# Loading x ahead of adj, first chunk two blocks at a time, and single loads behind each tanh, in a two-layer graph kernel on one core

## The reference

```
filt = tanh(adj * adj) * (adj > 0);  new_adj = the 350 largest of each row
h2   = tanh(x @ W_proj + b_proj);    x1 = layernorm(x + relu(new_adj @ (h2 @ W_gcn) + b_gcn))
node = [(adj > 0) @ x1, (adj < 0) @ x1] @ node_W + node_b * diag(adj)
edge = (adj @ x1) @ edge_W + edge_b * diag(adj)
out  = layernorm(x1 + node + edge)
```

## Time and profile before

| | |
|---|---|
| median of three runs | 616.18 us |
| the profiled execution, its time and its span | 615.21 us, 613.4 us |
| PE busy | 603.1 us, 98% of the span |
| DVE, ACT, POOL busy | 471.4, 418.2, 186.8 us |
| DMA | 130.65 MB, mean 213 GB/s |
| granted TensorE clock | 0.999 of full |

### The profile page before, as it was taken

One profiled execution on the slowest core, in us unless ns is written; L12 is line 12 of the kernel. 1 busy time (PEld: TensorE's weight loads), 2 busy tenths in 40 slices (PEclk: granted clock), 3 DMA queues, 4 the chain that ended last, 5 costly groups with the idle time before them and its releaser, 6 DMA issues.

```text
span 613.4 us, 5755 instructions
## 1 busy us (share of the span) xinstructions
PE 603.1 (98%) x1986; PEld 344.0 (56%) x1986; DVE 471.4 (77%) x681; ACT 418.2 (68%) x299; POOL 186.8 (30%) x80
## 2 busy tenths in 40 slices
PE   7999999999999999999999999999999999999996
PEld 6644444444444444455555655655655656557995
DVE  2677979788887979986787697796796786886743
ACT  2676786868687686648884783883983883875950
POOL 0398697888879797100000000000000000000000
PEclk9999999999999999999999999999999999999999
DMA  8999999999999980047898399388487595784000
GB/s 238 311 348 347 345 322 325 264 324 299 323 271 302 321 205 0 2 137 205 231 247 241 106 253 252 102 244 226 133 238 194 162 249 154 193 248 124 2 18 18
DMA packets 141181, 130.65 MB, mean 213 GB/s; under 512 B 9443, under 2 KB 141158, under 8 KB 141158
## 3 DMA queue, kind: packets, MB, share of 16 engines
q1 hardware_dynamic: 74982, 66.22, 38.8%
q10 hardware_dynamic: 66176, 64.17, 37.5%
HBM read 128.27 MB, written 2.10 MB: 213 GB/s over the span
## 4 chain that ended last, share of the span: by engine, by line
PE 97%; DMA 1%; SPq 0%; ACT 0%; DVE 0%; issue 0%; ACTq 0%; DVEq 0%
PE acc L988 36%; PE acc L1002 34%; PE stage L1011 10%; PE stage L1010 10%; PE stage L1002 2%; PE to_rows L1017 1%; PE to_rows L1016 1%; DMA x_rows<-in_x_dram 1%; PE stage L956 1%; PE to_rows L973 1%; PE stage L962 1%; SPq L378 0%; PE to_rows L948 0%; PE to_cols L962 0%; PE stage L951 0%
## 5 line engine op out<-in xcount | busy, mean ns | idle before, releaser
L630 DVE STREAM_TRANSPOSE a_cols<-a_rows 128x2048 f32<-128x2048 f32 x128 | 294.6, 2306 | 91.9 <-PE stage L1011 53.0
L988 PE MATMUL acc<-a_cols,rhs 128*128 128x512 f32 x512 | 221.4, 592 | 0.8 <-ACT a_cols L559 0.7
L1002 PE MATMUL acc<-a_cols,x_rows 128*128 128x512 f32 (+1 forms) x512 | 216.2, 565 | 0.0
L367 POOL TENSOR_TENSOR a_cols<-a_cols 128x1536 f32<-128x1536 f32 x64 | 175.3, 2748 | 61.5 <-DVE a_cols L630 60.6
L988 PEld LDWEIGHTS acc<-a_cols,rhs 128*128 128x128 f32 x512 | 96.6, 190 | 119.9 <-issue 119.9
L559 ACT ACTIVATE a_cols<-a_cols 128x2048 f32<-128x2048 f32 x64 | 122.3, 1912 | 49.2 <-POOL a_cols L367 48.0
L1002 PEld LDWEIGHTS acc<-a_cols,x_rows 128*128 128x128 f32 x512 | 96.0, 189 | 86.3 <-issue 81.0
L579 ACT ACTIVATE a_rows<-a_rows 128x4096 f32<-128x4096 f32 x32 | 115.9, 3623 | 25.6 <-DVE a_cols L630 12.3
L1010 PE MATMUL stage<-masks,x_hi 128*128 128x512 f32 (+1 forms) x288 | 126.8, 449 | 0.0
L582 ACT ACTIVATE a_rows<-a_rows 128x4096 f32<-128x4096 f32 x32 | 116.0, 3624 | 1.0
L1011 PE MATMUL stage<-masks,x_lo 128*128 128x512 f32 (+1 forms) x288 | 103.1, 367 | 0.0
(11 more groups left out here) (107 smaller groups left out, 235.7 us busy)
## 6 DMA issues: line engine op xcount, KB each, us to landing
a_rows<-in_adj_dram ACTq DMA_DIRECT2D x120, 512.0 KB, 10.1
a_rows<-in_adj_dram SPq DMA_DIRECT2D x120, 512.0 KB, 9.0
out_dram<-n_rows SPq DMA_DIRECT2D x28, 64.0 KB, 8.4
x_rows<-in_x_dram ACTq DMA_DIRECT2D x6, 128.0 KB, 4.5
x_rows<-in_x_dram SPq DMA_DIRECT2D x6, 128.0 KB, 6.2
x_rows<-in_x_dram ACTq DMA_DIRECT2D x4, 64.0 KB, 2.2
x_rows<-in_x_dram SPq DMA_DIRECT2D x4, 64.0 KB, 2.1
diag<-in_adj_dram SPq DMA_DIRECT2D x16, 1.0 KB
```

Of the source, the lines that this page charges most:

```text
L367: nc.gpsimd.tensor_tensor(part, part, part, ALU.mult).then_inc(squared_pool, 1)
L630: nc.vector.transpose(half_out(hs), half_in(s, h % HALVES)).then_inc(turned[layer], 1)
L988: last = nc.tensor.matmul(acc[parity][:], rhs[:, b, :], a_cols[:, h % HSLOTS, k, :], start=(b == 0), stop=(b == BLOCKS - 1))
L1002: last = nc.tensor.matmul(sums, x_rows[:, b, :], rows(a_cols[:, h % HSLOTS, k, :]), start=(b == 0), stop=(b == BLOCKS - 1))
```

## The change

- x is loaded whole ahead of adj, in six parts of 4, 4, 4, 4, 8 and 8 blocks. W_proj goes ahead of part 1 on SP's queue; b_proj has a semaphore of its own; b_gcn moves from ACT's queue to SP's, behind the four pieces of chunk 0.
- The head runs its 8 groups in one regular order; the eight matmuls of ones are gone; DVE makes all copies of turned x, ACT one more copy of `rhs`. Two halves instead of three are turned before the head ends.
- In chunk 0 each half is worked as two pairs of blocks: two transposes, two squares on POOL and on ACT, two tanhs, and PE waits for each pair.
- From chunk 1 on ACT issues one quarter after each tanh, never two.
- At the end the last two tiles have a PSUM bank each; their sums are copied, weighed and taken into the statistics one by one.

Layer 1 up to its last two tiles is as before; apart from the ones no product with data is added or left out, and the bytes loaded are the same.

```diff
-X_PARTS = [4, 4, 8, 8, 8]
-X_FIRST = 4
+X_PARTS = [4, 4, 4, 4, 8, 8]
...
-KEEP_WARM = 8
-EARLY = [("rhs", 4), ("rhs", 5), ("rhs", 7)]
+PAIR = HB // 2
+PAIR_POOL = PAIR * CH * 3 // 4
+EARLY = [("rhs", 5), ("rhs", 6)]
...
-last_rows = [to_rows[:, 0:PARTS[0][1], :],
-             acc_m[1 - LAST[2]][:, 0:PARTS[1][1] * F].rearrange("p (t f) -> p t f", f=F)]
+last_rows = [[to_rows[:, k, :] for k in range(PARTS[0][1])],
+             [acc_m[1 - LAST[2]][:, 0:F], stats_at[:, 0:F]]]
...
 GROUPS = BLOCKS // TILES
-X_LAST = sum(X_PARTS[:X_FIRST]) // TILES
...
 USES = turns[:2]
-for k in range(X_LAST):
-    USES += hids[k:k + 1] + rhss[max(k - 2, 0):max(k - 1, 0)] + turns[:X_LAST][k + 2:k + 3]
-USES += rhss[X_LAST - 2:X_LAST - 1] + turns[X_LAST:X_LAST + 1] + rhss[X_LAST - 1:X_LAST] + turns[X_LAST + 1:]
-for k in range(X_LAST, GROUPS):
-    USES += hids[k:k + 1] + rhss[k - 1:k] * (k > X_LAST)
-USES += rhss[GROUPS - 1:]
-by_dve = [(k == "turn" and g < GROUPS - 1) or (k == "rhs" and g not in (1, 2, 3)) for k, g in USES]
+for k in range(GROUPS):
+    USES += hids[k:k + 1] + rhss[max(k - 2, 0):max(k - 1, 0)] + turns[k + 2:k + 3]
+USES += rhss[GROUPS - 2:]
+by_dve = [k == "turn" or (k == "rhs" and g not in (1, 2, 3, 4)) for k, g in USES]
...
     def layer0(chunk, before):
         for h in range(HPC):
+            if not before:
+                first, second = (pair(a_cols, h % HSLOTS, k)[:, 0:PAIR_POOL] for k in range(2))
+                pool.wait_ge(pair_turned, h + 1)
+                nc.gpsimd.tensor_tensor(first, first, first, ALU.mult).then_inc(pair_squared_pool, 1)
+                pool.wait_ge(turned[0], h + 1)
+                nc.gpsimd.tensor_tensor(second, second, second, ALU.mult).then_inc(squared_pool, 1)
+                continue
...
     load_x(0)
+    sp.dma_start(w_pg[:, 0, :], w_proj).then_inc(proj_loaded, 16)
     load_x(1)
-    sp.dma_start(w_pg[:, 0, :], w_proj).then_inc(proj_loaded, 16)
-    sp.dma_start(b_col[:, 0:1], b_proj.rearrange("(p a) -> p a", a=1)).then_inc(proj_loaded, 16)
-    for part in range(2, X_FIRST):
+    load_x(2)
+    sp.dma_start(b_col[:, 0:1], b_proj.rearrange("(p a) -> p a", a=1)).then_inc(b_proj_loaded, 16)
+    for part in range(3, len(X_PARTS)):
         load_x(part)
-    load_piece((0, 0), 0)
-    for part in range(X_FIRST, len(X_PARTS)):
-        load_x(part)
-    for s in range(1, PIECES):
+    for s in range(PIECES):
         load_piece((0, 0), s)
+    sp.dma_start(b_col[:, 1:2], b_gcn.rearrange("(p a) -> p a", a=1)).then_inc(b_gcn_loaded, 16)
...
     act.dma_start(w_pg[:, 1, :], w_gcn).then_inc(gcn_loaded, 16)
-    for part in range(3, X_FIRST):
+    for part in range(3, len(X_PARTS)):
         load_x(part)
     load_piece((0, 0), 0)
-    for part in range(X_FIRST, len(X_PARTS)):
-        load_x(part)
-    act.dma_start(b_col[:, 1:2], b_gcn.rearrange("(p a) -> p a", a=1)).then_inc(b_gcn_loaded, 16)
-    act.wait_ge(proj_loaded, 32)
-    waiting = iter([(rows_of(0, chunk), s, q) for chunk in ((0, 0, 0), (1, 0, 1)) for s in range(PIECES)
-                    for q in ACT_QUARTERS][len(ACT_QUARTERS):])
-    def load_next():
-        load_quarter(*next(waiting))
...
+    def load_ahead(n):
+        c, at = divmod(n, PIECES * len(ACT_QUARTERS))
+        s, q = divmod(at, len(ACT_QUARTERS))
+        if c < CHUNKS:
+            load_quarter(rows_of(0, (c, c // 2, c % 2)), s, ACT_QUARTERS[q])
+    def first_half(h):
+        hs = h % HSLOTS
+        act.wait_ge(pair_turned, h + 1)
+        rest = pair(a_cols, hs, 0)[:, PAIR_POOL:]
+        nc.scalar.activation(rest, rest, ACT.Square).then_inc(pair_squared_act, 1)
+        act.wait_ge(pair_squared_act, h + 1)
+        act.wait_ge(pair_squared_pool, h + 1)
+        nc.scalar.activation(pair(a_cols, hs, 0), pair(a_cols, hs, 0), ACT.Tanh).then_inc(pair_tanh, 1)
+        act.wait_ge(turned[0], h + 1)
+        rest = pair(a_cols, hs, 1)[:, PAIR_POOL:]
+        nc.scalar.activation(rest, rest, ACT.Square).then_inc(squared_act, 1)
+        act.wait_ge(squared_act, h + 1)
+        act.wait_ge(squared_pool, h + 1)
+        nc.scalar.activation(pair(a_cols, hs, 1), pair(a_cols, hs, 1), ACT.Tanh).then_inc(tanh_done, 1)
     def square_rest(n):
...
-                load_next()
-            if g == 6:
-                square_rest(0)
-        elif kind == "turn":
-            nc.scalar.copy(group(feat_t, g), bank_of(n)).then_inc(stage_act, 1)
...
     def layer0(chunk, before):
         c = chunk[0]
+        if not before:
+            for h in range(HPC):
+                first_half(h)
+                load_ahead(HEAD_LOADS + h)
+            act.wait_ge(b_gcn_loaded, 16)
+            return
         for h in range(HPC):
-            if h == 2 and before:
+            if h == 2:
                 relu_out(before)
             n = c * HPC + h
...
-            if h % HALVES == HALVES - 1 and before and chunk is not LAST:
-                load_piece(rows_of(0, next_of(chunk)), h // HALVES)
-            if h or before:
-                square_rest(n)
-            if h == 7 and before:
+            square_rest(n)
...
-            if not before:
-                load_next()
-        if not before:
-            load_next()
+            load_ahead(HEAD_LOADS + n)
...
+    def turn_pairs(h):
+        s, hs = h // HALVES, h % HSLOTS
+        if h % HALVES == 0:
+            dve.wait_ge(a_loaded[s], 16 * QUARTERS)
+        if h >= HSLOTS:
+            dve.wait_ge(half_used[0], h + 1 - HSLOTS)
+        for k, signal in enumerate((pair_turned, turned[0])):
+            nc.vector.transpose(half_out(hs)[:, :, k * PAIR:(k + 1) * PAIR, :],
+                                half_in(s, h % HALVES)[:, :, k * PAIR:(k + 1) * PAIR, :]).then_inc(signal, 1)
     for n, (kind, g) in enumerate(USES):
         if not by_dve[n]:
             continue
         if (kind, g) in EARLY:
-            turn(0, 0, EARLY.index((kind, g)))
+            turn_pairs(EARLY.index((kind, g)))
...
-        nc.vector.tensor_copy(by_tile(sm_t[:])[:, :, at:at + tiles, :],
-                              last_acc_m[part][:, 0:tiles * P]
-                              .rearrange("f (q m i) -> f q m i", q=QUARTERS, i=SQ)).then_inc(sums_m_kept, 1)
+        cols = last_acc_m[part][:, 0:tiles * P].rearrange("f (q m i) -> f q m i", q=QUARTERS, i=SQ)
+        step = 1 if part else tiles
+        for k in range(0, tiles, step):
+            nc.vector.tensor_copy(by_tile(sm_t[:])[:, :, at + k:at + k + step, :],
+                                  cols[:, :, k:k + step, :]).then_inc(sums_m_kept, 1)
...
-        dve.wait_ge(rows_ready, 2 * CHUNKS + part)
...
-                for _ in range(KEEP_WARM):
-                    nc.tensor.matmul(bank[:, 0:P], ones[:], ones[:], start=True, stop=True)
             pe.wait_ge(x_loaded[part_with(g * TILES)], 16 * QUARTERS)
...
-            pe.wait_ge(tanh_done, n + 1)
+            if before:
+                pe.wait_ge(tanh_done, n + 1)
             for k in range(HB):
+                if not before and k == 0:
+                    pe.wait_ge(pair_tanh, h + 1)
+                if not before and k == PAIR:
+                    pe.wait_ge(tanh_done, h + 1)
                 b = h * HB + k
...
+            pe.wait_ge(stats_step, 5)
+            for k in range(tiles):
+                nc.tensor.matmul(last_rows[part][k], ident[:], y_rows[:, at + k, :], start=True, stop=False)
...
-            pe.wait_ge(sums_m_kept, CHUNKS + part)
             for k in range(tiles):
-                last = nc.tensor.matmul(last_rows[part][:, k, :], blk(sm_t, at + k), w_pne[:, 0, :],
-                                        start=False, stop=(k == tiles - 1))
-            last.then_inc(rows_ready, 1)
+                pe.wait_ge(sums_m_kept, CHUNKS + part + part * k)
+                last = nc.tensor.matmul(last_rows[part][k], blk(sm_t, at + k), w_pne[:, 0, :],
+                                        start=False, stop=(part == 1 or k == tiles - 1))
+                if part == 1 or k == tiles - 1:
+                    last.then_inc(rows_ready, 1)
```

47 lines of the change are left out of this document (33 added, 14 removed).

## The result

The changed kernel takes 611.32 us (median of 12 runs, 610.34 to 616.43) against 615.15 us for the one before, in runs on the same chip: a ratio of 0.9935, with a 95% interval of 0.9913 to 0.9957. That is 3.8 us or 0.65% faster, within the 1% that counts as no change here. The prediction was 610.9 us. The profiled execution took 611.06 us with a span of 609.3 us; before it was 613.4 us. The 4.1 us between the two spans are what the traces have to account for; each trace is one execution.

A forecast was written before the change was run, and what follows sets the result against it. PE was taken to bound the kernel, busy 603.1 of 613.4 us. Gains of 4.1 + 0.1 + 0.8 + 0.3 = 5.3 us gave 609.9, plus 0.97 for the median, 610.9 us; range 609.5 to 612.7.

The forecast's parts named there:

- the start of the stream: Head: PE's matmuls into acc start at about 24.1 instead of 28.18 us, 4.1 us earlier.
- its three terms: Upper side of the range: later x 1.1 us, waits on pairs 0.5, chunk 1's gain not coming 0.8.
- the second rival: Head: ACT is free sooner as issue stalls shrink, rhs some 0.8 us earlier at most; 610.1 us; chance 0.07.
- Piece 0: Head: the first piece of adj, 2.10 MB at 347 GB/s, lands at 17.3 instead of 19.10 us.
- The first rival: Head: a load, x's parts or piece 0, lands 2 to 3 us late and bounds the start; 613.3 us; chance 0.13.
- a cover of 3.4 us: Chunk 1's first piece lands at about 41.5, wanted at 51.9, steps take 7.0 us: 3.4 us cover b_gcn's delay.
- The prediction's own sign of being wrong: Wrong if PE waits on x or ACT within the head, or DVE waits on adj from chunk 1 on.
- Chunk 0: Ahead of chunk 0's later halves only 0.1 us was lost before; 0.1 us booked as won.
- Chunk 1: Start of chunk 1: single quarters on ACT let relu follow in time, removing PE's wait for z_t, 0.8 us.
- The end: Last two tiles: copying one tile lets PE start earlier, statistics run beside PE's second product; 0.3 us gained.
- The late second quarter: From chunk 1 on: landings over 15.2 us make DVE wait, each us more costs 7 us; 622.1 at 16.8; chance 0.05.
- The clock: Head: without the ones PE idles more and could fall to 1.2 GHz; up to 624 us; chance 0.03.

The follow-up runs named there:

- ACT's piece 1 earlier: Changed kernel with ACT's five quarters of the head each issued one hid earlier, none behind hid 7; 611.07 us, ratio 0.9926.
- ACT's quarters later: Changed kernel with each of ACT's quarters from chunk 1 on issued two tanhs later; 638.37 us, ratio 1.0301.
- whole halves, PE busy: Changed kernel with chunk 0 worked by whole halves, plus 20 matmuls of ones behind PE's head; 613.7 us, ratio 0.9963.
- x balanced: Changed kernel with the last part of x in three quarters by ACT's queue and one by SP's; 612.01 us, ratio 0.9949.
- b_gcn on POOL: The kernel of ACT's piece 1 earlier, with b_gcn's 128 packets of 4 bytes on POOL's queue at the start; 610.56 us, ratio 0.9912.
- whole halves: Changed kernel with chunk 0 transposed, squared and given its tanh by whole halves, as in the kernel before; 615.33 us, ratio 1.0004.
- ACT free at the first pair: Changed kernel with b_gcn on POOL's queue and ACT's quarter behind hid 7 moved behind the first pair's tanh; 611.32 us, ratio 0.9931.
- ACT's piece 1 later: Changed kernel with ACT's quarters of piece 1 issued only behind the tanhs of hid 5 and 6; 616.12 us, ratio 1.0.
- pairs only: Kernel before, with chunk 0 two blocks at a time and nothing else of the change; 616.28 us, ratio 1.0008.
- single quarters alone: Kernel before, with one quarter of adj per tanh on ACT in every chunk, nothing else of the change; 615.85 us, ratio 1.0011.
- the last two tiles only: Kernel before, with the last two tiles one by one, each with its own PSUM bank, nothing else changed; 615.73 us, ratio 1.0009.

## Why the prediction was right, and where it was not

- **The time** was right (610.9 against 611.32), and so was the forecast that it stays within 1%, but it came closer than the sum deserves. The sum gave 5.3 us of gain; the spans show 4.1 and the medians 3.8. The 0.97 us that I added for the median of three runs made up for most of that: the median of the kernel before is 615.15 us over 12 runs, not 616.18. That was luck. One term of the sum was 1.0 us too large, the start of the stream.
- **The range** of the forecast, up to 612.7 us, is less than its three terms added to 610.9 (1.1, 0.5 and 0.8 us: 613.3).
- **The start of the stream: 4.1 us predicted, 3.1 measured.** Its parts were off more than the sum. *ACT* was free at 8.16 us rather than 9.61: the stalls in its issues of x did shrink (its two adj issues took 1.01 us, and nothing stood behind them), which was the second rival. The first rhs came at 9.59 instead of 10.4. *PE* then took 13.35 us, as worked out (13.2), with no wait; but x's last part landed only 0.4 us ahead of the turn that reads it (14.46 and 14.85), not 4.6, and with ACT free at the first pair PE waited 0.40 us for it. *Piece 0* is the step that failed: it was to land at 17.3 us, and landed at 20.98, later than before.
- **Why piece 0 was late.** I divided bytes by the mean rate and took 347 GB/s from 11.2 us on. Two things came in between. First, 10 to 15 us moved only 257 GB/s, and ACT's queue, through with its half of piece 0 at 17.0 us, went on to piece 1; SP's had moved its share (half of x, W_proj and half of piece 0, 2.16 MB) at 18.7 us: 1.4 of the 3.7 us. Second, a mean rate gives the time at which an average engine is through, but a piece has landed when the last of the 16 is: from 18.7 to 20.98 us, the other 2.3 us. (The view tells queues apart, not engines; that single engines lag is my reading of the completions.) It is the same with x: the last part, put at 11.2 us, has the first of its last sixteen completions at 11.07 us and the last at 14.46. From x's last completion to piece 0's it takes another 6.5 us, about one piece at the full rate (6.0). This held in each kernel with the new order that kept both queues fed:

| | last of x | piece 0 | between |
|---|---|---|---|
| ACT's piece 1 earlier | 13.06 | 19.92 | 6.9 |
| ACT's quarters later | 13.46 | 20.17 | 6.7 |
| changed kernel | 14.46 | 20.98 | 6.5 |
| whole halves, PE busy | 14.47 | 20.72 | 6.3 |
| x balanced | 14.61 | 20.83 | 6.2 |
| b_gcn on POOL | 15.08 | 21.22 | 6.1 |
| whole halves | 15.46 | 22.01 | 6.6 |
| ACT free at the first pair | 15.82 | 22.10 | 6.3 |

  With ACT's piece 1 later, where ACT's queue ran dry, x landed at 13.21 and piece 0 at 22.39 us, 9.2 us behind it; the rule doesn't hold there. The trace of before showed such stragglers: the fourth part of x had completions from 7.3 to 12.5 us. The Trainium skill (DMA: Bandwidth & Descriptors, Why a DMA increments its semaphore by 16 and not by 1) says that a DMA runs on up to 16 engines that finish independently; the completions agree. That the last completion of x lags the first of the last sixteen by 1.7 to 4.4 us in these kernels, and by another amount in each execution, the runs show; why it does, they leave open. How much of the 1.4 us the balance between the queues is worth is not shown either, since x balanced made the other queue late.
- **Why 3.7 us at the landing cost only 1.0.** PE's head was to end at 24.1, and ended at 22.94; the first pair follows the landing within 4.1 us, so it came at 25.09. The pair's lower bounds were close: DVE 1.20 us (1.15), POOL 1.47 (1.4), tanh 1.06 (1.0). The first rival, a load that bounds the start, is what happened, at two fifths of its price (1.0 of 2.4 us).
- **More would not have counted.** Had acc started at 24.1, chunk 1 would have started at 52.95 all the same, as with ACT's piece 1 earlier: I put piece 4 at 41.5 us, and it landed at 45.75. Of these 4.2 us 3.7 are piece 0's, and most of the rest is b_gcn, which the prediction let delay piece 4 at no cost. The remark that a cover of 3.4 us would do was wrong: piece 4 is on the path. The prediction's own sign of being wrong, DVE waiting on adj from chunk 1 on, did appear (1.88, 1.54 and 1.53 us in chunk 1, none from chunk 2 on); so did DVE's wait for piece 0, which was not to be there.
- **Chunk 0: 0.1 predicted, 0.02 measured.** Before, 0.36 us were lost in chunk 0 (27.90 against the 27.54 without any wait). The pairs close them (pairs only: 27.54), and the wait for piece 4 opens them again (27.88), 0.17 us of it as the idle time of one row.
- **Chunk 1: 0.8 predicted, 0.82 measured.** ACT's quarters are single rows of 0.32 us, and the wait is gone, in the changed kernel and with single quarters alone. The Trainium skill (DMA: Bandwidth & Descriptors, Issuing engines are not separate DMA queues) calls the issue time usually small; these rows differ: two issues held ACT for 5.09 us. Not all of that was on PE's path, as I had written, but the 0.80 us that PE waited.
- **The end: 0.3 predicted, 0.33 measured,** and seen again in the trace with the last two tiles only.
- **The late second quarter** did not come: from chunk 3 on ACT's last quarter of a piece lands 10.1 to 11.4 us after its issue, and pieces land 2.6 to 5.1 us ahead of DVE (5.9 to 10.5 us before); in chunk 2 the least is 0.9 us. Its direction was right, as the kernel with later quarters shows. Its price of 7 us for each us is not tested, since that edit shortened the loop to 4 halves. The landing of up to 15.2 us that the rival allowed agrees with the loop: 6 halves are 20.8 us, less 5.4 for transpose, square and their gaps leave 15.4.
- **The clock** stayed at 1.00 in the traced execution, and its mean is 0.997 to 1.000 in all 12 runs, but my reason was too weak. I argued from one window in which PE was half busy. In four neighbours of the changed kernel it fell around a wait of PE: 2.84 us (0.66 in the window that follows), 4.77 us (0.56), 5.63 us (0.77) and 4.46 us (0.50). In the first three it cost 1.7 to 2.6 us of chunk 0. In the changed kernel and in the one with ACT free at the first pair PE waits 2.16 and 2.15 us, and it held. The Trainium skill (TensorE: Matmul & The Clock Gate, HAM oscillation) has an idle PE fall back to half rate; these rows agree. But the longest wait alone doesn't decide it. With single quarters only, in the head with the ones, PE was busy 2.36 of 4 us at 5 to 9 us, with waits of up to 1.29 us, and the clock was 0.51 in 9 to 12 us. The kernel before was busy for 1.78 of the same 4 us, waited 1.64 us, and had 1.00. So rows much like the ones I argued from came out the other way. With whole halves the wait was 5.63 us and the clock fell, so the shorter wait that the pairs leave goes with a clock that held; but x balanced has pairs too, and there it fell. A chance of 0.03 was too low.

## What to carry to other kernels

A load has landed when its slowest engine is through: while both queues are fed, take the last completion of its predecessor in the trace, add the transfer at the full rate, and don't divide all bytes by a mean rate. When a start is moved forward, work out the next landings too, since the second one bounds what the first has freed (here 7.2 us before chunk 1). Where matmuls that keep the clock up are taken out, look at the waits that remain on PE and at the clock of several runs, not of one window.

## What the hardware showed that I had not expected

- One queue nearly alone moved 214 GB/s while the engines showed 99.8% busy, two moved 345. Holding back one queue's loads to favour the other's made both late (piece 0 at 22.39 us, piece 1 at 30.28; 20.98 and 26.95 in the changed kernel).
- The issue of one quarter of adj took 0.32 us in most rows, but up to 3.63 us in some, and two took 5.71 us (20.82 and 20.65 us above); what stands behind it on that engine starts later. That the queue was full then is my reading; no view shows it.
- The same loads of x, issued in the same order, landed up to 2.4 us apart in the traces of six kernels (last of x 13.06 to 15.46 us). Piece 0 followed 6.3 to 6.9 us later in the five that kept both queues fed.
- 128 packets of 4 bytes in SP's queue between pieces 3 and 4 put piece 4 back by 0.5 us in five of seven kernels, by 1.2 us in one and not at all in one.
